# First image of a convolution kernel: x loaded ahead of the factors, its statistics shared by ScalarE and VectorE, the first weight difference on GpSimd and two scaled parts on ScalarE

## What is computed

```
def _gn(v, G=32, eps=1e-5):
    m = mean(v by group);  s = var(v by group)
    return (v - m) / sqrt(s + eps)

# layer 0
v = round(clip(_gn(x) * input_factor, -1, 1) * 127) / 127 * 0.6
fv = patches(v) + 0.1 * patches(v) ** 3
outs = [conv3x3(fv, (g_pos - g_neg)[i]) for i in range(3)]
mem = 4 * adc(outs[0]) + 2 * adc(outs[1]) + 2 * adc(outs[2])   # adc: scale, round, clip
x = x + mem * output_factor + bias
# layer 1
q, k, v = Wq @ _gn(x), Wk @ _gn(x), Wv @ _gn(x)
x = x + Wm @ (q * (exp(B) @ (exp(k) * v)) / (exp(B) @ exp(k)))
```

## Time and profile before

| what | us |
|---|---|
| median of three runs | 1584.97 |
| lowest and highest of them | 1582.66, 1585.08 |
| the profiled execution's own time | 1582.16 |
| its span, first to last instruction | 1580.4 |
| busy: PE, DVE, ACT, POOL | 1456.5, 1390.4, 1162.4, 503.9 |
| first matmul of the convolution | at 57.44 |

### The profile page before, as it was taken

One profiled execution on the slowest core, in us unless ns is written; L12 is line 12 of the kernel. 1 busy time (PEld: TensorE's weight loads), 2 busy tenths in 40 slices (PEclk: granted clock), 3 DMA queues, 4 the chain that ended last, 5 costly groups with the idle time before them and its releaser, 6 DMA issues.

```text
span 1580.4 us, 22708 instructions
## 1 busy us (share of the span) xinstructions
PE 1456.5 (92%) x7792; PEld 622.2 (39%) x7792; DVE 1390.4 (88%) x2165; ACT 1162.4 (74%) x1511; POOL 503.9 (32%) x505
## 2 busy tenths in 40 slices
PE   1499999999999999999999999999999999999864
PEld 1254434344443434444344433434443443444322
DVE  3879899998989899998989998898999989898646
ACT  4357778786877878787778878787777878776444
POOL 2221324242433333333333333333342423424212
PEclk9699999999999999999999999999999999999987
DMA  5010111313222231323113132311313132111231
GB/s 201 1 54 15 40 28 40 108 41 107 54 60 75 55 107 28 107 54 91 49 49 107 28 107 56 98 49 41 107 28 111 50 107 54 41 41 41 67 80 54
DMA packets 29173, 103.80 MB, mean 66 GB/s; under 512 B 4032, under 2 KB 4224, under 8 KB 29056
## 3 DMA queue, kind: packets, MB, share of 16 engines
q1 hardware_dynamic: 20416, 70.86, 12.2%
q0 software_dynamic: 8640, 31.46, 10.5%
HBM read 37.29 MB, written 33.55 MB: 45 GB/s over the span
## 4 chain that ended last, share of the span: by engine, by line
PE 74%; DVE 18%; issue 4%; ACT 2%; POOL 1%; DMA 0%; DVEq 0%; SPq 0%; POOLq 0%; ACTq 0%
PE A L476 13%; PE A L478 12%; PE A L477 12%; PE L L536 7%; PE B L476 7%; PE B L478 7%; PE B L477 7%; PE L L580 4%; PE L L567 3%; DVE uall L1069 1%; DVE duo L987 1%; ACT junk L707 1%; DVE A L1039 1%; DVE duo L1036 1%; DVE uall L1042 1%
## 5 line engine op out<-in xcount | busy, mean ns | idle before, releaser
L476 PE MATMUL A<-T,WH 128*128 128x504 f16 (+1 forms) x1152 | 439.8, 382 | 1.0 <-ACT uall L731 1.0
L477 PE MATMUL A<-T,WH 128*128 128x504 f16 (+1 forms) x1152 | 438.2, 380 | 0.0
L478 PE MATMUL A<-T,WL 128*128 128x504 f16 (+1 forms) x1152 | 438.0, 380 | 0.0
L1308 POOL TENSOR_TENSOR T<-t,T 128x512 f16<-128x512 f32 x192 | 245.6, 1304 | 412.5 <-ACT T L689 412.5
L707 ACT ACTIVATE junk<-xr,shift 128x1024 f16<-128x1024 f32 x256 | 293.9, 1148 | 12.4 <-DVE xr L1072 5.2
L1282 POOL TENSOR_TENSOR zl<-z,zh 128x512 f16<-128x512 f32 x120 | 150.9, 1277 | 398.8 <-ACT zh L764 397.8
L476 PE MATMUL B<-T,WH 128*128 128x504 f16 (+1 forms) x576 | 221.2, 384 | 29.6 <-POOL T L1308 20.5
L478 PE MATMUL B<-T,WL 128*128 128x504 f16 (+1 forms) x576 | 220.3, 382 | 0.9 <-issue 0.9
L477 PE MATMUL B<-T,WH 128*128 128x504 f16 (+1 forms) x576 | 220.5, 383 | 0.0
L476 PEld LDWEIGHTS A<-T,WH 128*128 128x128 f16 x1152 | 115.3, 100 | 196.1 <-issue 83.8
L478 PEld LDWEIGHTS A<-T,WL 128*128 128x128 f16 x1152 | 112.9, 98 | 136.9 <-issue 1.1
(11 more groups left out here) (153 smaller groups left out, 2449.0 us busy)
## 6 DMA issues: line engine op xcount, KB each, us to landing
xr<-in_x_dram SPq DMA_DIRECT2D x64, 512.0 KB, 5.8
out_dram<-xr SPq DMA_DIRECT2D x64, 512.0 KB, 2.7
xr<-shared POOLq DMA_DIRECT2D x60, 512.0 KB, 4.6
xr<-in_L_conv_g_pos_dram SPq DMA_DIRECT2D x3, 576.0 KB, 9.9
xr<-in_L_conv_g_neg_dram SPq DMA_DIRECT2D x3, 576.0 KB, 11.2
xr<-in_L_conv_Wm_dram SPq DMA_DIRECT2D x2, 32.0 KB, 10.4
xr<-in_L_conv_Wq_dram SPq DMA_DIRECT2D x1, 32.0 KB, 11.2
xr<-in_L_conv_Wk_dram SPq DMA_DIRECT2D x1, 32.0 KB, 10.9
```

Of the source, the lines that this page charges most:

```text
L476: nc.tensor.matmul(to, wh, th, start=fresh and y == 1, stop=False, skip_group_check=True)
L477: nc.tensor.matmul(to, wh, tl, start=False, stop=False, skip_group_check=True)
L478: done = nc.tensor.matmul(to, wl, th, start=False, stop=y == 2, skip_group_check=True)
L1308: last = nc.gpsimd.tensor_tensor(low, t32[:, pair, :, :, :].rearrange("p t e w -> p (t e w)"), high, ALU.subtract)
```

## The change

Nothing in the phases changes. In the head for image 0:

- SP issues all four quarters of x first, then the two transfers of weight plane 0, then the three factors, then planes 1 and 2.
- ACT sums quarters 0 and 2 only (`head_stats_x`). DVE handles quarters 1 and 3 with `bn_stats` on four pieces of 512 elements and turns the result into the same kind of sums (`head_sums`: four `bn_stats`, one `bn_aggr` and four operations on one value per partition, and a memset).
- The weight difference of plane 0 moves from DVE to POOL, where it stands ahead of `scale_x`; those of planes 1 and 2 move behind `scale_x`.
- `half` and `right` of plane 0 move from DVE to ACT (`first_scaled`), behind ACT's statistics. DVE makes the rest of the sums, with `quantise` of quarter 0 between the first four operations and the last two.
- On ACT `level` and `cubic` of quarter 2 stand ahead of `high_weights` of plane 0. On DVE `cubic_f` of quarter 2 stands ahead of the three `low_weights`.

ACT's first instruction is the scaling of `inf` as before, with its wait for all three factors.

```diff
-            load(0, 0, 0)
+            for g in range(NG):
+                load(0, 0, g)
+            for t, src in ((gp, gp_v), (gn, gn_v)):
+                sp.dma_start(t[:, 0:CK], src[:, 0, :]).then_inc(g_loaded[0], 16)
             sp.dma_start(inf[:, :], in_factor.partition_broadcast(P)).then_inc(factors_loaded, 16)
             sp.dma_start(bcol[:, :], bias.rearrange("(c a) -> c a", a=1)).then_inc(factors_loaded, 16)
             sp.dma_start(outf[:, :], out_factor.partition_broadcast(P)).then_inc(factors_loaded, 16)
-            for g in range(1, NG):
-                load(0, 0, g)
-            for i in range(NP):
+            for i in range(1, NP):
...
+            def head_stats_x(q):
+                act.wait_ge(loaded[q], 16)
+                if q == 0:
+                    nc.scalar.activation(shift[0][:, :], xr[0][:, 0:1], ACT.Identity, scale=-1.0).then_inc(shifted[0], 1)
+                    act.wait_ge(shifted[0], 1)
+                else:
+                    act.wait_ge(stats_in[0], q)
...
+            def first_scaled():
+                d = tap_weights(0)
+                act.wait_ge(w_diff, 1)
+                for k in range(2):
+                    nc.scalar.activation(parts[:, k], d[:, 1 + k], ACT.Identity, scale=-CSCALE / 6
+                                         ).then_inc(first_parts, 1)
...
-            for q in range(NG):
-                stats_x(0, 0, q, (0, 0, q - 1) if q else ())
+            head_stats_x(0)
+            head_stats_x(2)
+            first_scaled()
             level(0, 0, 0)
             level(0, 0, 1)
             cubic(0, 0)
             cubic(0, 1)
-            high_weights(0)
             level(0, 0, 2)
             cubic(0, 2)
+            high_weights(0)
...
+                    dve.wait_ge(first_parts, 2)
                 stt(out=left, in0=d[:, 0], scalar=-CSCALE / 6, in1=right, op0=ALU.mult, op1=ALU.add
...
+                if not i:
+                    quantise(0, 0)
                 stt(out=U[:, i, 2], in0=half, scalar=-0.5, in1=far, op0=ALU.mult, op1=ALU.add)
...
+            head_sums()
             spread_stats(0, 0)
             group_moments(0, 0)
-            dve.wait_ge(g_loaded[0], 32)
-            nc.vector.tensor_tensor(gp[:, 0:CK], gp[:, 0:CK], gn[:, 0:CK], ALU.subtract).then_inc(w_diff0, 1)
             weight_sums(0)
-            quantise(0, 0)
...
             transform(0, 0, ())
+            cubic_f(0, 2)
             for y in range(3):
                 low_weights(0, y)
-            cubic_f(0, 2)
...
+            weight_difference(0)
+            scale_x(0)
             weight_difference(1)
             weight_difference(2)
-            scale_x(0)
```

More of the change, by code:

```diff
@@ L170, in conv_layers_kernel @@
         chan = two("chan", [P, 1])
+        hst = sb("hst", [P, NG, 6])
+        hmv = sb("hmv", [P, 2])
+        hch = sb("hch", [P, 1])
         gin = two("gin", [P, GROUP + 1])
@@ L227, in conv_layers_kernel @@
         const_step = sem("const_step")
-        w_diff0 = sem("w_diff0")
         w_diff = sem("w_diff")
@@ L233, in conv_layers_kernel @@
         parts_made = sem("parts_made")
+        first_parts = sem("first_parts")
+        head_stats = sem("head_stats")
+        head_moments = sem("head_moments")
         sums_made = sem("sums_made")
@@ L421, in phase @@
                 if isinstance(p, int) and p == 1:
-                    sp.wait_ge(w_diff0, 1)
-                    sp.wait_ge(w_diff, NP - 1)
+                    sp.wait_ge(w_diff, NP)
                     sp.wait_ge(small_turned, 1)
@@ L690, in rows_high @@
                                    ).then_inc(th_ready, 1)
+            def head_stats_x(q):
[5 more added lines that the diff above has]
+                    act.wait_ge(stats_in[0], q)
+                for k, func in enumerate((ACT.Identity, ACT.Square)):
+                    if k:
+                        act.wait_ge(passed[0], q + 2)
+                    nc.scalar.activation(junk[:, :], xr[0][:, q * PX:(q + 1) * PX], func, bias=shift[0][:, :],
+                                         accum_out=moments[0][:, k, q:q + 1]
+                                         ).then_inc(stats_in[0] if k else passed[0], 2)
+            def first_scaled():
[4 more added lines that the diff above has]
+                                         ).then_inc(first_parts, 1)
             def channel_stats(which, src, image, q, before):
@@ L885, in weight_sums @@
                 half, right, left, far = (parts[:, k] for k in range(4))
+                dve.wait_ge(w_diff, i + 1)
+                made = 4 * i - 2
+                stt = nc.vector.scalar_tensor_tensor
                 if i:
-                    dve.wait_ge(w_diff, i)
                     dve.wait_ge(sums_made, i)
-                else:
[L890 to L895, removed]
+                    nc.vector.tensor_scalar(half, d[:, 1], -CSCALE / 6, None, ALU.mult).then_inc(parts_made, 1)
+                    nc.vector.tensor_scalar(right, d[:, 2], -CSCALE / 6, None, ALU.mult).then_inc(parts_made, 1)
+                    dve.wait_ge(parts_made, made + 2)
+                else:
+                    dve.wait_ge(first_parts, 2)
                 stt(out=left, in0=d[:, 0], scalar=-CSCALE / 6, in1=right, op0=ALU.mult, op1=ALU.add
@@ L923, in small_low, with head_sums @@
                                                ).then_inc(small_done, 1)
+            def head_sums():
+                count = 2.0 * PX
+                nc.vector.memset(moments[0][:, :, 3], 0.0).then_inc(head_moments, 1)
+                for i, q in enumerate((1, 3)):
+                    dve.wait_ge(loaded[q], 16)
+                    for h in range(2):
+                        at = q * PX + h * HALF
+                        nc.vector.bn_stats(hst[:, 2 * i + h, :], xr[0][:, at:at + HALF]).then_inc(head_stats, 1)
+                dve.wait_ge(head_stats, NG)
+                nc.vector.bn_aggr(hmv[:, :], hst[:, :, :].rearrange("p a b -> p (a b)")).then_inc(head_stats, 1)
+                dve.wait_ge(head_stats, NG + 1)
+                dve.wait_ge(shifted[0], 1)
+                nc.vector.tensor_scalar(hch[:, :], hmv[:, 0:1], shift[0][:, :], None, ALU.add).then_inc(head_stats, 1)
+                dve.wait_ge(head_stats, NG + 2)
+                nc.vector.tensor_scalar(moments[0][:, 0, 1:2], hch[:, :], count, None, ALU.mult).then_inc(head_moments, 1)
+                nc.vector.scalar_tensor_tensor(out=hmv[:, 0:1], in0=hch[:, :], scalar=hch[:, :], in1=hmv[:, 1:2],
+                                               op0=ALU.mult, op1=ALU.add).then_inc(head_stats, 1)
+                dve.wait_ge(head_stats, NG + 3)
+                nc.vector.tensor_scalar(moments[0][:, 1, 1:2], hmv[:, 0:1], count, None, ALU.mult).then_inc(head_moments, 1)
+                dve.wait_ge(head_moments, 3)
             def spread_stats(which, image):
```

## The result

The changed kernel takes 1579.42 us (median of 8 runs, 1575.99 to 1580.86) against 1583.51 for the kernel before (8 runs, 1582.42 to 1585.08, the three of the table before among them). The ratio is 0.9965 with a 95% interval of 0.9954 to 0.9975: 4 to 7 us faster. The forecast was 1578 in 1573.5 to 1583. The sign and the range held; the head, on which the sum was made, did not come out as summed.

What follows compares the result with a forecast made beforehand. TensorE bounds the kernel after the head, so only the convolution's first matmul counts: 5.4 + 0.95 = 6.3 us won, 51.1 instead of 57.44. From different baselines this gave 1575.9, 1577.4 or 1578.7; 1578 was taken, range 1573.5 to 1583.

Steps and rivals of the forecast that it cites:

- rival (c): In the head's loads: factors land as late as plane 0 did plus 0.8, at 15.7; 2.7 us won, 1582.3; chance 0.11.
- F: Time at which the factors have landed and ACT starts: forecast 12.1, low end 11.3, high end 15.7.
- part 1: Load order: factors behind x and plane 0 make ACT start at 12.1, 4.7 us later than before.
- part 2: ACT's statistics in the head: four passes instead of eight take 5.2 us and end at 17.6, 0.4 before the old 18.04.
- part 3: Group statistics: L937 takes 0.22 us instead of 2.08, so 2.5 us remain of 4.3; variance at 20.1 against 22.3.
- part 4: scale_x on POOL: 3.6 us, bounds 1.75 and 4.1; level starts at 23.7 against 26.52, 2.8 us won.
- part 5: Behind scale_x: POOL's differences stall DVE, sums complete at 30.1; transform 6.0 us earlier, rows_high 37.8 against 43.18, 5.4 won.
- parts 5 and 6: Reorderings: transform at 33.45 against 39.46, no longer behind high_weights; cubic_f ahead of low_weights makes rows_low 3.41 instead of 4.36.
- (b): Rival: POOL and DVE don't collide behind scale_x; sums done at 26.3, 10.1 us won, 1574.9; chance 0.18.
- (d): Rival: matmuls start earlier but a later wait or longer half-clock stretch takes it back; 1583 to 1586; chance 0.08.
- (e): Rival: factors not served until planes 1 and 2 are through, landing about 21; slower, about 1587.5; chance 0.03.

Runs made afterwards that it cites:

- e1: The kernel before with the two reorderings alone (level and cubic of quarter 2, cubic_f of quarter 2 moved ahead): 1580.29 us, ratio 0.9977 to the kernel before.
- e6: The changed kernel with the old load order (first quarter of x, factors, rest), SP waiting for DVE's statistics before image 1: 1577.14 us, ratio 0.9944.
- e8: The kernel before with the two reorderings alone, run again beside the changed kernel: 1578.31 us, ratio 0.9967 to the kernel before.
- e3: The changed kernel with ACT's wait for the factors behind its statistics, SP waiting for DVE's statistics before image 1: 1571.66 us, ratio 0.9924.
- e4: The changed kernel with the weight differences of planes 1 and 2 on DVE, no longer on POOL: 1575.22 us, ratio 0.9946 to the kernel before.
- e2: The changed kernel with the two reorderings undone: 1585.03 us, ratio 1.0005 to the kernel before.
- e9: The changed kernel with ACT's factor wait behind its statistics and planes 1 and 2's differences on DVE, second run: 1567.53 us, ratio 0.9892.

## Why the prediction was right or wrong

The range and the sign were right. The gain was forecast as 6.3 us and is 4.1 by the medians, 5.5 by the ratio; of the head, 3.4 us of the 6.3 came. What came is the landing of rival (c) (F at 15.3, forecast chance 0.11), for which the forecast had 2.7 us of head and 1582.3. That the time lies near 1578 all the same is in part luck. The kernel before came out 1.5 us faster than the 1584.97 that the forecast started from, and the ratio gives the changed kernel 2 us more than its head does. The head's miss of 3.0 us adds up from the profile within 0.2 us: 3.2 for the factors, 0.2 for ACT's passes and 0.6 for the transposes (7.4 us and not 6.8; why they took longer isn't shown), less 0.7 at scale_x and 0.2 at the collision. Point by point:

- **The load order (part 1).** This is the step that failed. I had ACT start at 12.1; it started at 15.30. Plane 0 came nearly as summed (POOL took it up at 12.34, forecast 11.3). The other 2 us are the 0.8 for the factors themselves: they took 3.0 behind plane 0, more than the 2.6 that I had as the upper bound (1.9 to 3.2 in the other eight profiles with this order). The last factor landed at 4.81 + 10.5 = 15.3, the one ahead of it at 4.30 + 8.5 = 12.8. In the kernel before the last factor was 2.2 us behind the one ahead of it too, in e1, e6 and e8 only 1.0 to 1.2. e6 and e3 price the late factors: 5.0 us of head by the load order, 7.5 by where ACT waits for them. The rule that the prediction weighed, of the Trainium skill (DMA: Bandwidth & Descriptors, "Queues, rings and completion order"), that a count lands behind the same DMA engine's earlier writes, is in line with this trace: plane 0 landed at 3.29 + 8.9 = 12.2, the first factor at 3.81 + 8.5 = 12.3, and nothing overtook.
- **Half of the statistics (part 2).** Four passes ended 5.7 us behind ACT's start (forecast 5.5) at 21.04 (17.6). The bn_stats took 1.29 for two of 512, as estimated, and were covered by 5 us of idle time. The two scaled parts took 1.64 instead of 1.0, also covered.
- **The group statistics (part 3).** Right: 0.22 us for the instruction that took 2.08.
- **scale_x (part 4).** 2.9 us where I took 3.6; the waits of POOL's small steps were shorter than summed (0.62, 1.00 and 0.52 us for the first three, against 0.23, 0.57 and 0.19 in e3, where DVE is idle beside them).
- **The collision (part 5).** Right in mechanism and nearly in size: 6.2 us from level's start to the end of the sums, forecast 6.4. e4 shows it by taking POOL's work away. But other instructions waited than I had: quantise for the first difference, L938 for the second, and L939, which I had waiting, ran in 0.55. The rule of the Trainium skill (SBUF — State Buffer, "Who interferes with whom") that quantise is shut out too agrees with the trace, and my sum, which let it run, does not: 1.48 us here, 0.43 in e4, 2.84 in e3. It cost little, since two differences cost DVE two waits either way.
- **The reorderings (parts 5 and 6).** Right: the transform at 35.8 instead of 39.46 in spite of statistics 3 us late, rows_low 3.37 for 4.36. e1 and e2 give them 5.2 to 6.0 us of head, all of the gain and more. The prediction didn't say so: it summed the change as one path and never asked what would be left of the gain if only the reorderings were done. Its sentence that the loads of image 1 wait for statistics that end no later was wrong too, these loads start at 18.29 and not at 12.51; PE's waits show no price for it.
- **The rivals.** (b) was ruled out by the changed kernel's own rows and by e4. Of (d) the later wait didn't come: from 50 to 200 us PE waits 5.8 us for low_weights before the change and 5.9 after it, and for the rest within 0.3 us as before. The longer stretch at half clock isn't settled: behind the first matmul the same kernel scatters by up to 2.8 us, as much as the head's miss. (e), the factors behind the other planes, didn't occur.

## What to carry to other kernels

When bulk transfers are moved ahead of tiny ones, look for whoever waits on the tiny ones first: here a wait that needed one value at the end of a 10 us stretch stood at its beginning, and moving it took 7.5 us off the head, twice what the whole change had taken. An elementwise operation moved from VectorE to GpSimd to relieve VectorE can cost VectorE more than it saves, when VectorE is the one on the path: the two differences held it up by 3.5 us here (1.05 at quantise, 2.4 at L938), against 2.7 us for doing both itself, and e4 put these off the head's path. A change of several parts should be summed for each part alone, too: one of them can hide what another loses.

## What the runs showed of the hardware

- In the kernel with the reorderings alone (e1) an instruction with a single tensor input was shut out as well: a tensor_scalar of 128 x 4 values took 2.34 us beside POOL's difference, where it took 0.23 in the kernel before. The same happened in e6 (2.51) and e9 (2.50). DVE's and POOL's timelines of e1:

```profile
17.55 0.22 DVE L937 SCALAR_TENSOR_TENSOR gin<-total,mean 128x1 f32<-128x1 f32 x1
17.69 0.21 DVE L940 TENSOR_SCALAR chan<-mean,shift 128x1 f32<-128x1 f32 x1
17.93 2.34 DVE L943 TENSOR_SCALAR gin<-mask,chan 128x4 f32<-128x4 f32 x1
...
17.64 2.61 POOL L1247 TENSOR_TENSOR xr<-xr 128x1152 f32<-128x1152 f32 x1 [13.94 <-DMA xr<-in_L_conv_g_neg_dram]
```

- The third of three transfers of 128 x 4 bytes landed 2.5 us behind the second, in the changed kernel at 15.3 and 12.8, though it was issued only 0.5 us behind it. In all thirteen profiles it was 0.9 to 2.7 us behind. Why wasn't tried.
- Between a POOL and a DVE instruction that shut each other out the turn alternates: in the changed kernel quantise ran behind POOL's first difference, the second difference behind quantise (2.79 us for it, where one alone takes 2.61), and L938 behind the second.
- The same kernel differs by up to 2.8 us from one profile to another in what lies behind the first matmul (0.2, 2.7 and 2.8 in three pairs), with different stretches at half clock; a gain of 1 to 3 us in a head can't be read from single executions.
